# One step of its own for each token tile's two indirect transfers, in a convolution, attention and expert kernel

## What is computed

```
x = x + _L0_conv_ref(_gn(x), L0_conv_weight)
t = _to_tokens(x)
t = t + _L1_attn_ref(_ln_t(t), L1_attn_Wq, L1_attn_bq, L1_attn_Wk, L1_attn_bk, L1_attn_Wv, L1_attn_bv)
t = t + _L1_ffn_ref(_ln_t(t), L1_ffn_gate_w, L1_ffn_gate_b, L1_ffn_w1, L1_ffn_w2, L1_ffn_w3)
x = _from_tokens(t, x)
```

## Time and profile before

| | us |
|---|---|
| median of 3 runs | 2852.15 |
| lowest and highest run | 2850.76 to 2854.89 |
| span of the profiled execution | 3215.9 |

### The profile page before, as it was taken

The page is one execution under the profiler, slowest core; times in us unless marked ns, Lnnn a source line. Parts: engine busy times, 40 slices in busy tenths (PEclk is TensorE's granted clock), DMA queues, the critical chain, the costliest instruction groups (busy, mean ns, idle before and its releaser), DMA issues.

```text
span 3215.9 us, 46697 instructions
## 1 busy us (share of the span) xinstructions
PE 2711.4 (84%) x13821; PEld 1688.8 (53%) x13821; DVE 1835.6 (57%) x5227; ACT 1312.9 (41%) x2985; POOL 1019.4 (32%) x1097
## 2 busy tenths in 40 slices
PE   4899988999989898998889889998999888775653
PEld 2455544665556555555556555555556544433442
DVE  4567755666657566565657656665656645522222
ACT  1344433554445444444445444544445443332221
POOL 2022034003331353224431353324431343343444
PEclk8899999999999899998999999999999999876565
DMA  2143001111111111212111111211111111122222
GB/s 62 29 92 76 24 29 43 31 37 46 43 47 43 47 55 49 49 38 58 44 48 43 48 53 49 48 39 50 49 46 34 39 46 45 35 50 60 68 68 43
DMA packets 226556, 152.97 MB, mean 48 GB/s; under 512 B 100240, under 2 KB 216720, under 8 KB 226320
## 3 DMA queue, kind: packets, MB, share of 16 engines
q1 hardware_dynamic: 192208, 98.97, 12.1%
q0 software_dynamic: 31456, 48.03, 6.2%
q10 hardware_dynamic: 2656, 2.98, 0.4%
HBM read 83.92 MB, written 65.27 MB: 46 GB/s over the span
## 4 chain that ended last, share of the span: by engine, by line
PE 59%; issue 10%; DVE 10%; another core or an unknown queue 5%; ACT 2%; POOL 1%; DMA 1%; SPq 0%; ACTq 0%; POOLq 0%; DVEq 0%
PE ps_o L1441 14%; PE ps_s L1429 8%; PE ps_m L1401 7%; PE ps_s L1430 6%; PE ps_x L1588 5%; PE ps_z L1603 3%; DVE max_part L1080 3%; PE ps_z L1467 3%; PE ps_z L1573 2%; PE ps_x L1596 2%; PE ps_s L1588 2%; PE ps_y L1504 1%; PE ps_y L1520 1%; PE ps_m L1603 1%
## 5 line engine op out<-in xcount | busy, mean ns | idle before, releaser
L1080 DVE TENSOR_REDUCE max_part<-ps_m 128x1 f32<-128x448 f32 x1400 | 858.8, 621 | 875.9 <-PE ps_m L1401 602.4
L925 ACT ACTIVATE prob<-ps_s 128x448 f32<-128x448 f32 x1400 | 756.2, 544 | 681.4 <-PE ps_s L1430 522.0
L1441 PE MATMUL ps_o<-prob,v_s 128*64 128x448 f32 x2800 | 718.3, 588 | 0.0
L1429 PE MATMUL ps_s<-q_a,k_a 128*128 128x448 f32 x1400 | 615.6, 440 | 85.1 <-issue 61.8
L1401 PE MATMUL ps_m<-k_a,q_a 128*128 128x448 f32 (+3 forms) x1600 | 547.6, 369 | 41.5 <-DVE max_part L1080 24.0
L767 POOL DMA_INDIRECT got<-sorted_y,slot x448 | 426.3, 952 | 377.6 <-issue 137.5
L1430 PE MATMUL ps_s<-q_b,k_a 128*128 128x448 f32 x1400 | 527.0, 376 | 0.0
L746 POOL DMA_INDIRECT sorted_x<-xn,slot x448 | 432.0, 964 | 292.0 <-issue 177.1
L785 POOL TENSOR_TENSOR ln_s<-ln_s,minus_half 112x4 f32<-112x4 f32 x56 | 58.0, 1036 | 1271.3 <-DVE ln_s L990 1240.6
L1429 PEld LDWEIGHTS ps_s<-q_a,k_a 128*128 128x128 f32 x1400 | 275.0, 196 | 251.3 <-issue 122.6
L1401 PEld LDWEIGHTS ps_m<-k_a,q_a 128*128 128x128 f32 (+1 forms) x1600 | 307.6, 194 | 119.7 <-DVE max_part L1080 68.9
(11 more groups left out here) (186 smaller groups left out, 3115.0 us busy)
## 6 DMA issues: line engine op xcount, KB each, us to landing
fx<-sorted_x SPq DMA_DIRECT2D x43, 384.0 KB
sorted_y<-fy SPq DMA_DIRECT2D x42, 320.0 KB
xh<-in_x SPq DMA_DIRECT2D x96, 126.0 KB, 2.7
fx<-sorted_x SPq DMA_DIRECT2D x47, 256.0 KB
sorted_x<-fy POOLq DMA_DIRECT2D x28, 320.0 KB, 6.0
sorted_x<-xn,slot POOLq DMA_INDIRECT x448
got<-sorted_y,slot POOLq DMA_INDIRECT x448
x_now<-in_x SPq DMA_DIRECT2D x112, 56.0 KB, 2.3
```

What stands on the lines that cost most here:

```text
L925: a.activation(prob[(at.n * KEY_TILES + i) % PROBS][:], ps_s[(at.n * KEY_TILES + i) % 2][:, 0:CHUNK], ACT.Exp).then_inc(s["p_ready"], 1)
L1080: v.tensor_reduce(max_part[n % 2][0:here.stop - here.start, j, kb:kb + 1], ps_m[(passes_before(n) + m) % 2][0:here.stop - here.start, 0:CH ...
L1429: t.matmul(ps_s[t_of % 2][:, 0:CHUNK], k_a[p][:, keys], high, start=True, stop=False)
L1441: t.matmul(ps_o[side:side + CHANNELS, 0:CHUNK], v_s[u % 2][:, i, :], prob[(n * KEY_TILES + i) % PROBS][:], start=(i < 2), stop=(i >= KEY_T ...
```

## The change

Only POOL's program changes; the other engines issue the same instructions in the same order. Rows are gone. `MOVES_AT` gives a step to each token tile of a list of 4, 8 or 12, and a list of 16 is spread evenly over steps 0 to 22. POOL waits for that step's scores and issues the tile's two transfers. `norm2` comes at step 7 (in the order of the list, without a wait for the step) instead of first, `norm1` at step 11, and the group norm's power, in an image's last chunk, at step 14. Each chunk keeps its list of tiles in the same order.

```diff
-ROW, ROWS_AT = 3, (8, 13, 18, 23)
+NORM2_AT, NORM1_AT, RSTD_AT = 7, 11, 14
+MOVES_AT = {4: (13, 16, 19, 22), 8: (1, 4, 8, 12, 15, 17, 19, 21), 12: (0, 2, 4, 8, 10, 12, 14, 16, 18, 20, 22, 24)}
...
-    def row(self):
-
-        return max(ROW, -(-len(self.moves()) // len(ROWS_AT)))
+    def moves_at(self):
+
+        many = len(self.moves())
+        return MOVES_AT[many] if many in MOVES_AT else [i * (KEY_TILES - 1) // many for i in range(many)]
...
+                events = []
                 if at.active("post"):
-                    norm2(at)
-                row = at.row()
-                later = row if len(at.moves()) > row and (at.c or at.moves()[0][0] == "gather") else 0
-                if later == 0 and at.active("pre"):
-                    norm1(at)
-                for place, (kind, chunk, j) in enumerate(at.moves()):
-                    if later and place == later and at.active("pre"):
+                    events.append((NORM2_AT if at.attends else -1, 0, "norm2", None, None))
+                if at.active("pre"):
+                    events.append((NORM1_AT, 0, "norm1", None, None))
+                if at.active("stats") and at.c == CHUNKS - 1:
+                    events.append((RSTD_AT, 0, "rstd", None, None))
+                events += [(step, 1) + move for step, move in zip(at.moves_at(), at.moves())]
+                for step, _, kind, chunk, j in sorted(events, key=lambda event: event[:2]):
+                    if kind == "norm2":
+                        norm2(at)
+                    elif kind == "norm1":
                         norm1(at)
-                    if place % row == 0 and at.attends:
-
-                        wait_apart(pool, s["s_done"], ONE + at.n * KEY_TILES + ROWS_AT[place // row])
-                    if kind == "scatter":
-                        scatter(chunk, j)
+                    elif kind == "rstd":
+                        group_rstd(at.u + 2)
                     else:
-                        gather(chunk, j)
+                        if at.attends:
+
+                            wait_apart(pool, s["s_done"], ONE + at.n * KEY_TILES + step + 1)
+                        if kind == "scatter":
+                            scatter(chunk, j)
+                        else:
+                            gather(chunk, j)
```

More of the change, by code:

```diff
@@ L814, in body @@
                         zero(*ZEROS[k])
-                if at.active("stats") and at.c == CHUNKS - 1:
-                    group_rstd(at.u + 2)
             group_rstd(0)
```

## The result

The median is 2857.16 us (20 runs, 2851.07 to 2862.9) against 2852.18 of the kernel before beside it (20 runs, 2847.77 to 2856.83): a ratio of 1.0016, 95% interval [1.0009, 1.0023]. The change costs 5 us. The prediction had 2851, a change of -1, and a range of 2815 to 2868, which holds the result.

The account below looks back on a forecast made before the run. The prediction took the kernel as PE-bound (TensorE busy 84% of 3215.9 us), with stops at rows of six mostly the recording's own. Spacing -6 and norm2 behind transfers +5 summed to -1 us: 2851 us, range 2815 to 2868.

Parts of the forecast that it names:

- norm2 behind transfers: Second chunks of five images: POOL's second-norm pow, behind six more transfers, comes late; 1 us each, +5 us.
- The term for spacing: Tiles' transfers spread over each chunk instead of rows of six: 0.6 of 10 us of stalls relieved, -6 us.
- the excess of 258 us: Chunks with transfers up to the attention's end: extra time in the profiled execution, held to be mostly the recording's own.
- The estimate of 236 us for the end of a timed run: End of the program after the last attention chunk: 2852 - 2616 = 236 us in a timed run, 342 in the profile.
- The 10 us of excess: Stalls with transfers: the part taken to be in timed runs too, 10 us out of a possible 0 to 47.
- That page's sum in the prediction: Whole kernel, if transfers and compute can't slow each other: no gain from spreading, +5 us, 2857.
- The 1.1 us to spare: Quiet chunk: from DVE applying the second norm (1020.61) to PE's transposes (1021.72), slack before a late pow costs PE.
- DVE's own delay: Images' second chunks: DVE runs late by up to 1.5 us after a combine awaiting its load, hiding the pow's lateness.
- The bound of 17 us: Five second chunks: upper cost of the late pow, twice 8 us, if each stop also lowers PE's clock.
- Later ends, earlier starts, waits: Last scatters 4.9 us later with 4 us to spare before PE's use; earlier gathers and added semaphore waits: all free.
- The first, stalls in the timed runs: Rows of six: stalls partly in timed runs, so spreading wins 15 to 40 us, 2812 to 2837; chance 0.29.
- The second, that POOL's queue loses more than it gives: Images' second chunks: pow behind fourteen transfers, no excess to relieve, +8 to +17 us, 2860 to 2869; chance 0.17.

Follow-up runs that it names:

- the second recording: The kernel before, unchanged, profiled a second time and timed beside the kernel before; ratio 1.0005 [0.9995, 1.0015].

## Why the prediction was wrong, point by point

The forecast was -1 us, and the kernel became 5 us slower. The step that turned the sign is the price of norm2 behind transfers: +5 us were taken, and the runs show 14. The term for spacing, -6, has a size near what was won, but by luck: the gain is at another place, for another reason.

**Which execution.** Right in substance: the excess of 258 us was held to be nearly all the recorded execution's own, and the second recording of the same program has a span of 2844.1 us without it. Against the second recording the excess is 282 us up to the attention's end, where 258 were summed up, and 90 behind it. The estimate of 236 us for the end of a timed run stands against 252 recorded. The 10 us of excess that were taken to be in timed runs aren't there: no row with "remote" is left in before or after.

**Spacing, -6 us.** This step failed too: a right size for a wrong reason. The third chunks of five images, twelve tiles each, take 224.6 us in before with rows of six and 224.8 in after, so there was nothing for the spreading to relieve. What the change does win, some 7 us, comes from the lists of sixteen, which this step had set aside as bunches that stay. The prediction looked there for transfers that stop other engines, and not for what stands behind them on POOL's own queue: the last chunk's pow.

The Trainium skill, "SBUF — State Buffer", section "SBUF: two separate sides", says that transfers and compute don't slow each other. The equal third chunks agree with it; the stops of the earlier trace rows belonged to one recording. That page's sum in the prediction, +5 us and 2857, is the measured time, but by accident: two terms beside it were off and cancelled.

**norm2 behind transfers, +5 us.** The mechanism and its place are right, the size isn't. POOL was to be free at 20.0 us into the chunk, 19.7 by the later start; in chunk 36 it is free at 19.7 (1713.68 - 1693.96), just as forecast. Four things made it dearer.

- The 1.1 us to spare were counted from the norm's last DVE instruction to the transposes. But these wait for `q_b`, the DVE instruction behind it, and from its end 0.6 us are left in before (1711.76 to 1712.35).
- DVE's own delay was to hide up to 1.5 us in these chunks. In before the variance is ready at 18.7, 17.8, 17.4, 17.0 and 15.4 us in chunks 22, 29, 36, 43 and 50 (16.9 in the quiet chunk of the earlier trace rows, by the same start): the combine at the start has mostly been made up by step 7. Only in chunk 22 did the cover hold: 47.28 us became 47.79. In chunk 36, of DVE's 2.98 us of waiting, 2.2 are new, and PE waits 1.79.
- Chunk 50 has no `pre` stage for a next image, so its steps are shorter. Its variance is ready 15.5 us in and the pow starts at 19.65: DVE waits 4.81 us, PE 3.63. The prediction counted five like chunks. Chunk 8 was counted as free by the variance of the quiet chunk, 16.9 by this start; there it is ready at 16.4 and POOL is free at 18.0, and the chunk takes 40.10 us for 38.48.
- The clock. Three of five chunks lost part of their full clock after the stop. PE's idle time alone grew by 8.2 us in the five chunks, 1.6 each, and its busy time by 9.9. The bound of 17 us had this in, the value taken hadn't.

In the profile that makes 18.1 us, and 1.6 for chunk 8. In the timed runs it is 14 by the difference of after (1.0016) and the kernel with both pows as before (0.9966); the pow's place alone, in rows, gave 8 (1.0028). Why the clock fell in fewer of those chunks there than in after isn't settled. The price goes by the medians: the recordings differ elsewhere too, by the clock.

**Later ends, earlier starts, waits: free.** Right. The five chunks after the last scatters, whose tokens SP loads next, take as long in after as in before (225.8 and 226.0 us together). In the closest of seven, chunk 32 of after, the load lands 3.1 us before PE wants it. And the kernel that keeps the later scatters, the first gathers and all the waits is the one at 0.9966.

**The rivals.** The first, stalls in the timed runs, fell with the second recording. The second, that POOL's queue loses more than it gives, is what happens in the second chunks, at 14 of its 8 to 17 us; it missed the time because it had "no excess to relieve" on the other side, where POOL's queue gave back 7. The sum as measured: +14, -7, and some -2 that can't be told from 0, is the +5. The predicted point was nearer than its terms.

**What would show it.** The pow directly behind fourteen transfers is there, with waits of DVE of 2 us and more in four of the five chunks (1.73 in chunk 22), and the loads aren't late. Second chunks of 55 us were too much (47.7 to 51.5), and so were third chunks near 48 (45.8 and less), most likely because both start from the earlier trace rows, the disturbed recording. "Span falls, median stays" came true for the plainest reason: another execution was recorded.

## What to carry to other kernels

When a queue's program is reordered, look at each short instruction that others wait for and ask how long the queue is busy ahead of it, in each kind of chunk apart: here a pow of 1.05 us that came to stand behind 14 transfers instead of 8 cost some 14 us in all, and behind 12 nothing that the runs can tell apart. The count isn't what decides, though, but by how much the queue comes free after its input is ready: chunk 8 of after, with an earlier variance, lost 1.6 us behind 12. Look for the same pattern at the places that the change makes better, too; the row that gave it away is one with no idle time ahead of it on its engine and a long wait on the engine that wants it. And where a profiled execution is 12.8% longer than the timed runs, record it again before any of its stalls becomes a term.

## What had not been expected of the hardware

A program can be recorded with 212.1 us of waits for words that come late from PE, and the next recording of the same program has none. The Trainium skill, "NOTIFIC — the notification-queue block", section 7.1, says that the block which writes trace records holds its producers back rather than lose a record inside; the second recording shows at least that the program doesn't always bring this on, and no run here shows the counter that would prove the cause.

The clock answers the same stop in different ways. Chunk 45 has PE busy for 40.6 of 44.7 us in before, and idle for about 4 in every recording but the first. Its line by stretches in before:

```profile
2107.50:2152.22 44.72, 40.58 (x213) 23.91 (x212) 31.85 (x93) 19.79 (x43) 20.61 (x22) 1.00 0.20 55
```

The same chunk in the kernel with the spreading and both pows as before:

```profile
2111.13:2157.08 45.95, 42.08 (x214) 24.94 (x212) 31.50 (x93) 20.04 (x43) 19.63 (x20) 0.96 0.22 60
```

And in the kernel before with the lists of sixteen in rows from step 0, which changes nothing in this chunk:

```profile
2110.12:2157.88 47.76, 43.59 (x213) 25.26 (x212) 31.86 (x93) 20.03 (x43) 20.63 (x22) 0.93 0.23 61
```

The idle time is 4.1, 3.9 and 4.2 us; the granted clock is 1.00, 0.96 and 0.93, and the chunk 1.2 and 3.0 us longer. The timed runs of after differ in the same way: the one of 2851.07 us had a mean granted clock of 0.963, the one of 2862.9 us 0.959. So one recording tells the length of a chunk with such a stop to 3 us only, and a sum over chunks has to be tested by medians.
